# Graph network kernel: one index table in place of four, first transposes ahead of the ranges, edge groups from doubled keys

## The reference, cut to what matters

```
src, dst = edges with self loops, dst sorted
deg = segment_sum(1, dst);  norm = rsqrt(deg)[src] * rsqrt(deg)[dst]
h   = x @ W                                     # 1250 x 768 x 768
x1  = layernorm(x + segment_sum(h[src] * norm, dst) + b)
out = layernorm(x1 + two attention layers(x1))  # 4 heads of 256, then 1 head of 768
```

## Time and profile before

| | |
|---|---|
| median of three runs | 1024.36 us (1019.54, 1024.36, 1024.40) |
| profiled execution, its own time | 1019.75 us |
| its span, first to last instruction | 1017.9 us |
| mean granted TensorE clock | 0.94 of full speed |
| busy: PE, DVE, ACT, POOL | 85%, 72%, 31%, 9% |
| index tables of L482 | 7.1 us, 4 instructions |
| groups of edge tiles in the loop | 44 |

### The profile page before, as it was taken

The page is one execution under the profiler, slowest core; times in us unless marked ns, Lnnn a source line. Parts: engine busy times, 40 slices in busy tenths (PEclk is TensorE's granted clock), DMA queues, the critical chain, the costliest instruction groups (busy, mean ns, idle before and its releaser), DMA issues.

```text
span 1017.9 us, 13650 instructions
## 1 busy us (share of the span) xinstructions
PE 862.4 (85%) x4888; PEld 544.8 (54%) x4888; DVE 733.8 (72%) x1182; ACT 312.7 (31%) x535; POOL 90.4 (9%) x92
## 2 busy tenths in 40 slices
PE   2799888889889989965999967879998989899781
PEld 2455555455555434422888856756555556455440
DVE  6678777778756668894677788785966542588887
ACT  0332322241002011113677655661122000444430
POOL 4000000100100003441000000001110000000001
PEclk9799999989999999987999989979999999899796
DMA  7000000213231012313230023110122624101112
GB/s 257 1 1 2 1 2 1 99 43 122 87 157 42 27 60 91 134 62 97 76 99 26 26 68 93 52 37 21 42 93 87 256 82 156 63 1 62 62 62 89
DMA packets 22611, 72.26 MB, mean 71 GB/s; under 512 B 2595, under 2 KB 3339, under 8 KB 22303
## 3 DMA queue, kind: packets, MB, share of 16 engines
q1 hardware_dynamic: 20030, 61.01, 17.3%
q0 software_dynamic: 2528, 10.55, 3.1%
HBM read 51.22 MB, written 20.33 MB: 70 GB/s over the span
## 4 chain that ended last, share of the span: by engine, by line
PE 29%; issue 25%; DVE 20%; POOL 3%; ACT 2%; DMA 2%; POOLq 0%; DVEq 0%; ACTq 0%; SPq 0%
PE psum L796 11%; PE psum L615 9%; PE psum L769 8%; DVE arena L1173 7%; DVE arena L1274 2%; DVE arena L1278 2%; DVE arena L1141 1%; DVE arena L1183 1%; DVE arena L1297 1%; POOL arena L567 1%; ACT arena L929 1%; DMA arena<-as_scratch 1%; DVE arena L1305 1%; POOL arena L539 1%; ACT arena L941 1%
## 5 line engine op out<-in xcount | busy, mean ns | idle before, releaser
L615 PE MATMUL psum<-arena 128*128 128x512 f16 (+1 forms) x1080 | 228.9, 370 | 8.1 <-DVE arena L999 7.1
L796 PE MATMUL psum<-arena 128*128 128x257 f32 x800 | 184.9, 393 | 34.0 <-ACT arena L929 24.4
L861 ACT ACTIVATE arena<-psum 128x320 f16<-128x320 f32 (+5 forms) x140 | 83.0, 626 | 378.7 <-PE psum L615 120.7
L796 PEld LDWEIGHTS psum<-arena 128*128 128x128 f32 x800 | 156.7, 197 | 60.9 <-issue 26.1
L615 PEld LDWEIGHTS psum<-arena 128*128 128x128 f16 (+1 forms) x1080 | 105.4, 100 | 117.0 <-issue 8.8
L769 PE MATMUL psum<-arena 128*128 128x512 f16 x960 | 160.6, 330 | 2.4 <-ACT arena L929 2.4
L769 PEld LDWEIGHTS psum<-arena 128*128 128x128 f16 x960 | 94.9, 99 | 66.2 <-issue 2.9
L941 ACT ACTIVATE arena<-arena 128x640 f32<-128x640 f32 x160 | 119.6, 829 | 8.2 <-DVE arena L1278 7.0
L836 PE MATMUL psum<-arena 128*128 128x512 f16 x600 | 106.3, 341 | 15.0 <-DVE arena L1376 14.8
L861 ACT ACTIVATE arena<-arena 128x256 f16<-128x256 f32 (+2 forms) x84 | 50.5, 614 | 157.1 <-DVE arena L1387 74.3
L1173 DVE CUSTOM_DVE_ANT_0 arena<-arena 128x1280 bf16<-128x1280 bf16 x50 | 88.2, 1825 | 13.1 <-DMA arena<-as_scratch 13.1
(11 more groups left out here) (157 smaller groups left out, 625.8 us busy)
## 6 DMA issues: line engine op xcount, KB each, us to landing
arena<-in_L_gnn_W_dram SPq DMA_DIRECT2D x14, 384.0 KB, 5.6
r_scratch<-arena SPq DMA_DIRECT2D x10, 512.0 KB, 2.6
arena<-uv_scratch SPq DMA_DIRECT2D x16, 320.0 KB, 3.9
arena<-r_scratch SPq DMA_DIRECT2D x10, 512.0 KB, 3.7
x_scratch<-arena SPq DMA_DIRECT2D x10, 384.0 KB, 4.7
arena<-x_scratch SPq DMA_DIRECT2D x10, 384.0 KB, 3.5
r_scratch<-arena SPq DMA_DIRECT2D x10, 384.0 KB, 2.6
arena<-r_scratch SPq DMA_DIRECT2D x10, 384.0 KB, 4.0
```

Source lines behind the costliest of these rows:

```text
L615: ins = pe.matmul(o[:, a:b], part[:, k, ds(t * P, P)], w[:, k, a:b], start=(k == 0 and n == 0 and m == 0), stop=(k == kn - 1 and n == 1))
L796: last = pe.matmul(p_att[:, j, 0:HID + 1], pf[n % PSLOTS][:, j * P:(j + 1) * P], xl[ch % H][:, k, 0:HID + 1], start=(k == 0), stop=(k == T ...
L861: act.activation(out_, in_, ACT.Copy, scale=scale).then_inc(signal, 1)
```

## The change

Six edits, all ahead of the first aggregation.

- GpSimd makes one table of keys, for a tile's first block, and `lo_io` at the start of its queue, ahead of the identity matrices. VectorE makes the other three by adding 32, 64 and 96 to it, after the tiles' bounds and before it waits for the transposed keys. `IOTAS`, the number of tables that is waited for, becomes 8.
- `key_s` and `lo_s` hold the keys and low parts twice: as they are, and from ETP on displaced by one edge tile. They and `zero_h` lie at other addresses.
- A block starts at its true first tile. If that is odd, it is replaced by ETP - 1 + first, in the second copy. The shift of the keys covers both copies.
- TensorE's transposes of x tiles 0 and 1 stand between the bounds' matmuls (L588) and the ranges' matmuls (L593).
- VectorE's `low_counts(t - 1)` stand behind the third block of tile t in place of the second.
- Low counts and degrees of three tiles (`TAIL`), 7 to 9, come after the loop, since the second half of `key_s` lies where `c_lo` of tile 7 goes.

```diff
-IOTAS = 7 + SUBS
+IOTAS = 8
+TAIL = 3
...
-        zero_h = at(late_pos, [T * WD], f16)
-        lo_s = at(late_pos + T * WD * 2, [ETP], i16)
-        key_s = at(125 * KB, [ETP], i16)
+        zero_h = at(125 * KB, [T * WD], f16)
+        lo_s = at(late_pos, [2 * ETP], i16)
+        key_s = at(88 * KB, [2 * ETP], i16)
...
# GpSimd: ahead of ident
+            pool.iota(key_io[:, 0].rearrange("p (k w) c -> p k w c", k=T), [[KS, T], [1, WD], [0, 2]], base=0,
+                      channel_multiplier=0).then_inc(S["iotas"], 1)
+            pool.iota(lo_io, [[1, P], [0, 2]], base=0, channel_multiplier=0).then_inc(S["iotas"], 1)
...
-            for j in range(SUBS):
-                pool.iota(key_io[:, j].rearrange("p (k w) c -> p k w c", k=T), [[KS, T], [1, WD], [0, 2]], base=j * WD,
-                          channel_multiplier=0).then_inc(S["iotas"], 1)
...
# TensorE: between tile_rows and ranges_f (they stood ahead of project_nodes(0))
+            transposes(0)
+            transposes(1)
             pe.wait_ge(S["ranges_f"], 1)
...
-                    if j == 2 and 1 <= t < T - 1:
+                    if j == 2 and 1 <= t <= T - TAIL:
                         degrees(t - 1)
-            degrees(T - 2)
-            degrees(T - 1)
+            for t in range(T - TAIL, T):
+                degrees(t)
...
# VectorE
+            dve.wait_ge(S["iotas"], 1)
+            for j in range(1, SUBS):
+                dve.tensor_scalar(key_io[:, j], key_io[:, 0], float(j * WD), None, ALU.add).then_inc(S["dve"], 1)
             dve.wait_ge(S["keys_tr"], 1)
-            dve.tensor_copy(key_s, p_key[:, 0:ETP]).then_inc(S["dve"], 1)
-            dve.tensor_copy(lo_s, p_lo3[:, 0:ETP]).then_inc(S["dve"], 1)
+            for shift in range(2):
+                dve.tensor_copy(key_s[:, shift * ETP:(shift + 1) * ETP], p_key[:, shift:shift + ETP]).then_inc(S["dve"], 1)
+                dve.tensor_copy(lo_s[:, shift * ETP:(shift + 1) * ETP], p_lo3[:, shift:shift + ETP]).then_inc(S["dve"], 1)
...
-            dve.tensor_scalar(first_t, first_t, 2 ** 15 - 2, None, ALU.bitwise_and).then_inc(S["dve"], 1)
-            dve.wait_ge(S["dve"], steps_done(1))
...
-            dve.tensor_tensor(range_i[:, 0:NB], first_t, g_latest, ALU.min).then_inc(S["dve"], 1)
+            dve.tensor_tensor(first_t, first_t, g_latest, ALU.min).then_inc(S["dve"], 1)
+            dve.wait_ge(S["dve"], steps_done(1))
+            dve.tensor_scalar(odd, first_t, 1, None, ALU.bitwise_and).then_inc(S["dve"], 1)
+            dve.wait_ge(S["dve"], steps_done(1))
+            dve.scalar_tensor_tensor(range_i[:, 0:NB], odd, float(ETP - 1), first_t, ALU.mult, ALU.add).then_inc(S["dve"], 1)
...
-                    if j == 1 and 1 <= t < T - 1:
+                    if j == 2 and 1 <= t <= T - TAIL:
                         low_counts(t - 1)
...
-            low_counts(T - 2)
-            low_counts(T - 1)
+            for t in range(T - TAIL, T):
+                low_counts(t)
```

More of the change, by code:

```diff
@@ L159, in gnn_program @@
         assert T * NP * 2 == 25 * KB
-        assert (T * WD + ETP) * 2 <= 16 * 10 * T and pos >= late_pos + 16 * 10 * T
-        zero_h = at(late_pos, [T * WD], f16)
-        lo_s = at(late_pos + T * WD * 2, [ETP], i16)
-        key_s = at(125 * KB, [ETP], i16)
+        assert 4 * ETP <= 16 * 10 * T and pos >= late_pos + 16 * 10 * T
+        zero_h = at(125 * KB, [T * WD], f16)
+        lo_s = at(late_pos, [2 * ETP], i16)
+        key_s = at(88 * KB, [2 * ETP], i16)
         ring_key = [at(4 * KB + i * G * T * WD * 2, [GP, T * WD, 2], f16) for i in range(2)]
@@ L190, in gnn_program @@
         g_latest = at(30 * KB + 640, [NB], i32, 1)
+        odd = at(30 * KB + 800, [NB], i32, 1)
         wst0 = [at((70 + 3 * i) * KB, [D], f32) for i in range(KD)]
@@ L467, in _ @@
             pool.memset(dst_i[:, 2, :], PAD_DST).then_inc(S["pads"], 1)
+            loose = dict(channel_multiplier=0, allow_small_or_imprecise_dtypes=True)
+            pool.iota(key_io[:, 0].rearrange("p (k w) c -> p k w c", k=T), [[KS, T], [1, WD], [0, 2]], base=0,
+                      channel_multiplier=0).then_inc(S["iotas"], 1)
+            pool.iota(lo_io, [[1, P], [0, 2]], base=0, channel_multiplier=0).then_inc(S["iotas"], 1)
+            for c in range(2):
+                pool.iota(thr[:, c:c + 1], [[0, 1]], base=c * WD, channel_multiplier=WD,
+                          allow_small_or_imprecise_dtypes=True).then_inc(S["iotas"], 1)
+            pool.iota(t_io, [[1, EG * P]], base=0, **loose).then_inc(S["iotas"], 1)
             pool.memset(ident, 0.0).then_inc(S["ident_ok"], 1)
@@ L473, in _ @@
                                    pattern=[[-1, P + shift]], channel_multiplier=1).then_inc(S["ident_ok"], 1)
[L474 to L478, removed]
             pool.memset(x_sb[:, T - 1, :], 0.0).then_inc(S["pads"], 1)
-            pool.iota(lo_io, [[1, P], [0, 2]], base=0, channel_multiplier=0).then_inc(S["iotas"], 1)
-            for j in range(SUBS):
-                pool.iota(key_io[:, j].rearrange("p (k w) c -> p k w c", k=T), [[KS, T], [1, WD], [0, 2]], base=j * WD,
-                          channel_multiplier=0).then_inc(S["iotas"], 1)
             pool.memset(zero_h, 0.0).then_inc(S["iotas"], 1)
@@ L590, in _ @@
             last.then_inc(S["tile_rows"], 1)
[L591 to L594, removed]
             def transposes(t):
@@ L606, in transposes @@
                 last.then_inc(S["x_tr"], 1)
+            transposes(0)
+            transposes(1)
+            pe.wait_ge(S["ranges_f"], 1)
+            for c in range(2):
+                last = pe.matmul(p_rng[:, c * NB:(c + 1) * NB], span[:, c:c + 1], ident[0:NB, 0:NB], start=True, stop=True)
+            last.then_inc(S["ranges_t"], 1)
             def product(o, lhs, rhs, t, kn, width, ks=None):
@@ L658, in degrees @@
                 last.then_inc(S["deg_done"], 1)
-            transposes(0)
-            transposes(1)
             project_nodes(0, range(KD))
@@ L1013, in _ @@
             dve.tensor_reduce(tmm[:, 1, :], dst_f, axis=AX.X, op=ALU.max).then_inc(S["keys_prep"], 1)
+            dve.wait_ge(S["iotas"], 1)
+            for j in range(1, SUBS):
+                dve.tensor_scalar(key_io[:, j], key_io[:, 0], float(j * WD), None, ALU.add).then_inc(S["dve"], 1)
             dve.wait_ge(S["keys_tr"], 1)
-            dve.tensor_copy(key_s, p_key[:, 0:ETP]).then_inc(S["dve"], 1)
-            dve.tensor_copy(lo_s, p_lo3[:, 0:ETP]).then_inc(S["dve"], 1)
-            steps_done(2)
+            for shift in range(2):
+                dve.tensor_copy(key_s[:, shift * ETP:(shift + 1) * ETP], p_key[:, shift:shift + ETP]).then_inc(S["dve"], 1)
+                dve.tensor_copy(lo_s[:, shift * ETP:(shift + 1) * ETP], p_lo3[:, shift:shift + ETP]).then_inc(S["dve"], 1)
+            steps_done(SUBS + 3)
             dve.wait_ge(S["tile_rows"], 1)
@@ L1084, in one_hots @@
                 dve.reg_load(r1, range_i[0:1, b + NB:b + NB + 1])
-                first, end = dve.snap(r0, min_val=0, max_val=ETP - G), dve.snap(r1, min_val=G, max_val=ETP)
+                first, end = dve.snap(r0, min_val=0, max_val=2 * ETP - G), dve.snap(r1, min_val=G, max_val=2 * ETP)
                 with dve.Fori(first, end, G) as tile:
-                    g = nc.s_assert_within(tile, 0, ETP - G, skip_runtime_bounds_check_because="the loop ends at ETP at most, in steps of G from its start")
+                    g = nc.s_assert_within(tile, 0, 2 * ETP - G, skip_runtime_bounds_check_because="the loop ends at 2 ETP at most, in steps of G from its start")
                     def pairs(v, width):
```

## The result

| | before | changed |
|---|---|---|
| median | 1023.39 us (4 runs, 1019.54 to 1024.40) | 992.88 us (4 runs, 992.36 to 993.37) |
| ratio to before, 95% interval | | 0.9709 (0.9681 to 0.9736) |
| profiled execution: time, span | 1019.75, 1017.9 | 992.64, 990.8 |
| first counting block starts (first L639, after: L642) | 42.01 | 33.56 |
| last block closed (start of the last L648, after: L651) | 198.45 | 169.14 |

What follows compares the result with a forecast made beforehand. TensorE was taken to bound the counting loop, behind a front that is one chain. Gains 5.7 + 18.8 + 2.6 + 0.6 = 27.7 us gave 992.0 from 1019.75 or 996.7 from 1024.36; forecast 994, range 988 to 1001.

Steps and rivals of the forecast that it cites:

- The front: Chain up to the first projection, about the first 42 us: low halves of W0 ready at 27.7, before 33.40; 5.7 gained.
- then it ends near 6.75: VectorE's first conversion (L1004), taken as held by GpSimd's work: 5.24 us earlier, 7.22 becoming about 2.0.
- the upper bound of 6.9: Most the first conversion could gain, if not held at all: 7.22 to 0.35.
- The groups: Counting loop: blocks 9, 20, 26 and 33 need one group, not two; 44 become 40, 18.8 us gained.
- Low counts one block later: Counting loop, tiles 1 to 7: TensorE's 0.45 stop at the third block goes, less a new wait; 2.6 us gained.
- rival B: VectorE becomes the counting loop's bound; tiles stay at 14.58 or grow by 0.1; 994.6 to 1000.3, middle 997; chance 0.11.
- Tail of three: Tile 7's degrees leave the period of t = 8 and go behind the last block, covered by idle time; 0.6 us gained.
- The back part: All after the last block: no row changed, so a microsecond saved earlier is one of the end; 0 booked.
- The middle between two places: The kernel before's runs lie at two places 4.9 us apart, giving 992.0 or 996.7; the middle, 994, was forecast.
- Rival A: First conversion's slowness is not GpSimd's doing; the front gains 0.5, the whole 22.5; middle 999.6 us; chance 0.08.
- C: Groups don't fall below 44 because the start is still rounded; 18.8 lost, middle 1013 us; chance 0.02.
- D: Key comparisons lose their pairwise speed, 1.82 becoming 3.5 us; kernel slower, 1072 us; chance 0.02.

Runs made afterwards that it cites:

- x_low_later: The changed kernel with VectorE's low half of x tile t + 2 made behind a tile's third block instead of the second; 991.11 us, median of 4.
- before_again: The kernel before, unchanged, traced once more; 1022.25 us in the profiled execution.
- low_counts_back: The changed kernel with VectorE's low counts back behind the second block of a tile, degrees and tail of three staying; 992.46 us.
- changed_again: The changed kernel, unedited, traced once more; 993.15 us in the profiled execution.
- tables_only: The kernel before with the tables' edit alone: one table at the head of GpSimd's queue, three made by VectorE; 1017.67 us.
- tables_waits: The kernel before with all four tables, GpSimd waiting for each to be done before issuing the next; 1019.86 us.
- even_starts: The changed kernel with every block's start rounded down to an even edge tile again, 44 groups in place of 40; 1013.95 us.

## Why the prediction was right, by its steps

**The front: 5.7 forecast, 8.45 measured (42.01 to 33.56).** The step that was mis-sized is "then it ends near 6.75". I read the end of the slow conversion, 0.22 behind GpSimd's last operation, as if GpSimd's whole work had held it, and so took the middle value. It was held by the tables that follow each other without a gap. In the changed kernel GpSimd works on until 7.28, but with short operations, and the one table ends before the conversion's data have landed (L471 from 1.13 to 2.94, the conversion from 4.78); so it takes 0.36, which was the upper bound of 6.9 less a hair. The ranges ended at 19.14 in place of 20.5, the projection started at 26.14 in place of 27.7 (1.6 of the difference), and its length, which the prediction kept at 8.72, was 7.58 (1.1). That last part is no merit of the change: with the same front the length was 8.51 in x_low_later. The additions on VectorE took 0.78 for three, less than the 1.0 forecast, and were hidden, as were the added copies. The transposes ahead gave the 0.7 that was booked.

**The groups: 18.8 forecast.** Count (40) and mechanism were right. Its size depends on what it is measured against: 17.4 where the clock stays (four times 4.35), 22.6 where it falls each time. The first trace had one fall. That 18.8 fitted was luck of that trace; before_again, with two, paid about 19.8 for the same groups.

**Low counts one block later: 2.6 forecast, 1.4 measured** (low_counts_back against the changed kernel). The prediction named the wait that would take the place of the old one, and where; it booked 0.08 for it. It was 0.14 to 0.18 in four of the seven tiles (14.26 to 14.30 in place of 14.12) and 0.5 in two (14.63), where VectorE's restart after the shift came later: L1100 stood idle 1.40 ahead of tiles 3 and 6, where it was 1.04 ahead of the others. The wait for ScalarE's conversion ahead of it, which the prediction's chain began behind, is what x_low_later takes away. This is half of rival B.

**Tail of three: 0.6 forecast.** The gain is to be sought in tile t = 8: the prediction's terms give it 12.8 (14.58 less 0.7, 0.45 and 0.6), and it took 13.05, or 12.91 in changed_again. The cost is to be sought behind the last close, where the work of tile 7 went. From that close to the first matmul of the aggregation (L695, after: L696) it is 7.33 before and 7.32 after:

```profile
198.45:205.78 7.33, 1.76 (x45) 1.38 (x44) 2.94 (x8) 3.11 (x5) 4.38 (x5) 0.80 0.72 243
```

```profile
169.14:176.46 7.32, 2.11 (x64) 1.81 (x64) 3.00 (x9) 3.10 (x5) 4.39 (x5) 0.74 0.70 254
```

So the added work was covered, as forecast. No run has this edit by itself.

**The back part: 0 forecast, 2.2 lost.** TensorE was busy longer for the same work at a lower granted clock (0.93 for 0.94), as in before_again, where nothing was changed. The prediction had named a longer back part as a sign of being wrong; against this trace the sign came, and before_again takes its force away. It cancels most of what the front gave beyond the forecast: 5.7 + 22.0 = 27.7 was said, 8.45 + 20.86 - 2.2 = 27.1 came. The whole was right by terms that erred both ways. It was right against the trace only: between the medians lie 30.5 us (1023.39 to 992.88), since the traced execution of the kernel before was one of its quickest. The mechanisms were sound; that 994 came within 1.2 of the median is in part luck.

**The middle between two places** of the kernel before was a poor reading of three numbers. Its runs lie from 1019.5 to 1025.4 over all jobs, in no two places. The five traces with 44 groups (before, before_again, tables_only, tables_waits, even_starts) show two things that move it: second groups with or without a fall of the clock, and the back part. The changed kernel has the first source no more; its four runs lie within 1.0 us.

Rival A is out by tables_only, C by x40, D by L1101's unchanged 1.82.

## What to carry to other kernels

Where two engines pass one buffer back and forth for a whole step, count the steps before speeding them up: a second round costs both engines' idle time, and sometimes the clock as well. An operation that is far longer than others of its shape (7.22 against 0.35 here) may be a held one; look at what the other engine was issuing without a gap at that time, and cut, space or move that. And compare stage by stage: a total that fits can hide terms of 1 to 3 us in both directions, so trace the unchanged kernel twice before a term of that size is believed.

## What was not expected of the hardware

- Four GpSimd tables that follow one another without a gap kept VectorE's conversion out for all four (7.22 us); a wait between them let one VectorE operation in at each (1.47 and 1.83). Two memsets without a gap let VectorE in between them (tables_only, L1007 in 0.85).
- The opposite direction, in the changed kernel: GpSimd's two selections took 0.98 in place of 0.62 and its memset 0.94 in place of 0.73 while VectorE worked beside them. In four traces where the conversion began 0.03 to 0.13 behind the first selection the two took 0.73, and it was VectorE's third operation that waited (0.85 in place of 0.41).
- A pause of 2.76 us on TensorE before a second group was followed by a granted clock of 0.91 to 0.92 over the tile in some executions and 1.00 in others, for the same program.
- The back part of one program differed by 2.3 us between two executions, with TensorE busy 4.4 us longer and every other engine alike.
